# Expert stage of a fused AdaLN / DeltaNet / MoE kernel: three tiles of output rows ahead of the second half of the FF columns, the odd slot in the first half, pair rows numbered by partition

## The reference, cut to what matters

```python
capacity = int(1.25 * N * K / E) + 1                 # N = 2048, K = 2, E = 8: 641 slots
k_probs, k_idx = jax.lax.top_k(softmax(xf @ router_w.T), K)
k_probs = k_probs / jnp.sum(k_probs, axis=-1, keepdims=True)
...                                                  # rank of each (token, k) in its expert; rank >= capacity is dropped
buf = jnp.zeros((E, capacity, H)).at[flat_e, slot].add(dispatched)
h = jax.nn.silu(jnp.einsum('ech,ehf->ecf', buf, w1))        # w1: 8 x 128 x 512
out_buf = jnp.einsum('ecf,efh->ech', h, w2)                 # w2: 8 x 512 x 128
pair_out = out_buf[flat_e, slot] * keep[:, None]
combined = jnp.sum(pair_out.reshape(N, K, H) * k_probs[..., None], axis=1)
return combined.reshape(B, T, H) + x
```

## Time and profile before

| | us |
|---|---|
| median of 3 runs | 432.74 |
| the runs | 432.74, 430.11, 435.56 |
| span of the profiled execution, first to last instruction | 396.5 |
| span of the experts in it, first up to the last product's end | 295.65 to 374.3 |
| from there to the end | 22.2 |

### The profile page before, as it was taken

How to read it: one execution, slowest core, us unless ns; L and a number is a source line. 1 busy time by engine, 2 the same in 40 slices (tenths; PEclk the granted TensorE clock), 3 DMA queues, 4 the chain that set the end, 5 groups by cost and what they waited for, 6 DMA issues and landing times.

```text
span 396.5 us, 11509 instructions
## 1 busy us (share of the span) xinstructions
PE 262.7 (66%) x4483; PEld 206.4 (52%) x4483; DVE 218.4 (55%) x760; ACT 104.2 (26%) x212; POOL 169.8 (43%) x165
## 2 busy tenths in 40 slices
PE   2945777866757748558767586373139999999700
PEld 0534454765544637344556465262128888888600
DVE  5576374876591984773795755256323443333425
ACT  1325213335113145122235130001203333333200
POOL 1223234542348460437581336631622555555523
PEclk9965557558556567755665855555558999999955
DMA  7980000000001000001000000000122243532055
GB/s 243 337 317 0 2 3 2 7 2 2 2 12 49 3 2 2 3 3 42 17 3 2 2 3 29 29 4 0 40 92 77 94 137 92 151 94 80 25 170 156
DMA packets 18687, 23.08 MB, mean 58 GB/s; under 512 B 2535, under 2 KB 13048, under 8 KB 18642
## 3 DMA queue, kind: packets, MB, share of 16 engines
q1 hardware_dynamic: 16306, 18.17, 14.4%
q0 software_dynamic: 2336, 4.24, 3.3%
HBM read 11.83 MB, written 11.10 MB: 58 GB/s over the span
## 4 chain that ended last, share of the span: by engine, by line
PE 44%; issue 23%; DVE 15%; POOL 7%; DMA 5%; ACT 3%; SPq 1%; DVEq 1%; POOLq 0%; ACTq 0%
PE ps L1616 9%; PE ps L1633 9%; PE ps L1453 7%; PE ps L1348 5%; PE ps L1333 5%; PE ps L1418 3%; POOL arena L626 2%; PE ps L1499 2%; DMA wmod<-in_wmod 2%; DMA arena<-pair_out 2%; DVE x L1039 2%; POOL arena L647 1%; PE ps L1436 1%; POOL rstd L574 1%; DVE msk L1073 1%
## 5 line engine op out<-in xcount | busy, mean ns | idle before, releaser
L706 POOL DMA_INDIRECT pair_out<-arena,meta x40 | 39.0, 975 | 48.6 <-DVE arena L1275 38.9
L1333 PE MATMUL ps<-const,arena 128*128 128x128 f32 x125 | 25.6, 350 | 28.4 <-DMA arena<-dispatched 11.8
L881 ACT ACTIVATE arena<-ps 128x384 f32<-128x384 f32 x64 | 26.2, 439 | 61.8 <-PE ps L1616 56.3
L1453 PE MATMUL ps<-arena,kT 32*32 32x128 f32 x512 | 24.1, 380 | 23.2 <-DVE wts L1015 14.6
L591 POOL DMA_INDIRECT dispatched<-row,idx x32 | 31.6, 988 | 17.8 <-issue 10.1
L1616 PE MATMUL ps<-arena,w1t 128*128 128x257 f32 (+1 forms) x128 | 38.5, 456 | 1.1 <-DVE arena L1259 1.1
L636 POOL TENSOR_TENSOR s_mk<-s_sb,const 128x512 f32<-128x512 f32 x16 | 21.2, 1325 | 40.8 <-ACT s_sb L792 40.8
L1633 PE MATMUL ps<-w2t,arena 128*128 128x128 f32 x320 | 37.0, 275 | 0.0
L1633 PEld LDWEIGHTS ps<-w2t,arena 128*128 128x128 f32 x320 | 36.4, 192 | 0.0
L1333 PEld LDWEIGHTS ps<-const,arena 128*128 128x128 f32 x125 | 18.8, 178 | 32.4 <-DMA arena<-dispatched 11.8
L1418 PE MATMUL ps<-v,wts 32*32 32x9 f32 x2048 | 28.3, 191 | 7.3 <-issue 7.3
(11 more groups left out here) (173 smaller groups left out, 511.5 us busy)
## 6 DMA issues: line engine op xcount, KB each, us to landing
dispatched<-fill SPq DMA_DIRECT2D x12, 260.0 KB, 4.9
arena<-dispatched SPq DMA_DIRECT2D x9, 325.0 KB, 3.4
w1t<-in_w SPq DMA_DIRECT2D x8, 256.0 KB, 2.9
w2t<-in_w SPq DMA_DIRECT2D x8, 256.0 KB, 2.9
pair_out<-zero SPq DMA_DIRECT2D x4, 512.0 KB, 6.4
arena<-pair_out SPq DMA_DIRECT2D x4, 512.0 KB, 5.7
out<-arena SPq DMA_DIRECT2D x4, 256.0 KB, 2.3
const<-in_constants SPq DMA_DIRECT2D x1, 790.0 KB, 6.6
```

What stands on the lines that cost most here:

```text
L706: pool.indirect_dma_start(pair_d, bass.IndirectOffsetOnAxis(ap=meta[:, u, a, 0:1].bitcast(U32), axis=0), orow[:, u, a, :], None, bounds_ch ...
L881: a_.activation(hid[:, u, f, c0:c0 + cn], ps[:, k % 4, 0:cn], ACT.Silu).then_inc(hid_done[u].sem, 1)
L1333: return nc.tensor.transpose(out, in_, ident[0:in_.shape[0], 0:in_.shape[0]])
L1453: f = mm(ps[j * BLK:(j + 1) * BLK, 2 * (hg % 2) + w, hg // 2 * P:(hg // 2 + 1) * P], st[r, t * P + j * BLK:t * P + (j + 1) * BLK], mv_[r, ...
```

## The change

Each expert is done in another order on TensorE: five of the eight up products (the first half of the slots for all four f, and one of the second half), the output tiles 0 to 2, the transposes for the next expert, the other three up products, tile 3 with the odd slot's product, tile 4. The odd slot moves to column 0 of `bT` and `hid`, so the first half is 385 columns and the second 256, and its four operations on VectorE come ahead of row product 0. The transposes get the banks 4 and 5 and the output tiles a ring of two, 6 and 7: tile a waits for the row product of tile a - 2. VectorE copies `meta` and the transposes behind row product 2. The last loop step is written out: no ninth expert is loaded or transposed, and the scatter of the odd rows goes ahead of that of tile 4. In SyncE's queue the wait for the even expert's scatters goes ahead of the wait and load for `w1t[1]`. The id of a pair becomes `32 * p + 8 * g + 2 * t + k` for partition p, group g and tile t, so a partition's pairs of a group are one run of 4 KB in `pair_out`, at a step of 16 KB from partition to partition.

```diff
-CH = (CT + 1) // 2 * P
+FA = (CT + 1) // 2
+CH = 1 + FA * P
 NHALF = [(0, CH), (CH, CAP - CH)]
 FT = FF // P
+UPS = [(f, n) for n in range(2) for f in range(FT)]
+UPS_A = FT + 1
+LAST_AT = CT - 2
...
-    c[:, COL["pid"]] = (TOPK * tok + np.arange(TOPK)[None, None, :]).reshape(P, -1)
+    c[:, COL["pid"]] = (PAIRS // P) * r + np.arange(TG * TOPK)[None, :]
...
-    pair_v = pair_d.rearrange("(g t p k) c -> g p t (k c)", t=TG, p=P, k=TOPK)
+    pair_v = pair_d.rearrange("(p g n) c -> g p (n c)", g=GROUPS, p=P)
...
-            return ps[:, 4 + (u * CT + a) % 4, :]
+            return ps[:, 6 + (u * CT + a) % 2, :]
+
+        def rows_made(a):
+
+            return a + 1 + (a > LAST_AT)
...
+                outs_gone(0, i)
                 sp.wait_ge(up_ps[1].sem, up_ps[1].now(i))
                 sp.dma_start(w1t[:, 1, :], w1_v(i * 2 + 3)).then_inc(w1_in[1].sem, 16)
-                outs_gone(0, i)
...
-            next_slots(0, NE // 2 - 1)
-            outs_gone(0, NE // 2 - 1)
...
+            with pool.Fori(0, NE // 2 - 1) as i:
+                rows_out(0, i, 0, CT)
+                rows_out(1, i, 0, CT)
+            rows_out(0, NE // 2 - 1, 0, CT)
+            rows_out(1, NE // 2 - 1, 0, CT - 1)
             pool.wait_ge(s_lastR, 2)
             pool.indirect_dma_start(pair_d, ...)
+            rows_out(1, NE // 2 - 1, CT - 1, CT)
...
+                    for k, (f, n) in enumerate(UPS):
+                        c0, cn = NHALF[n]
+                        act.wait_ge(up_ps[u].sem, up_ps[u].now(i, k + 1))
+                        if k == 0:
+                            act.wait_ge(r_ps[u].sem, r_ps[u].before(i))
+                            act.wait_ge(last_done[u].sem, last_done[u].before(i))
+                        a_.activation(hid[:, u, f, c0:c0 + cn], ps[:, k % 4, 0:cn], ACT.Silu).then_inc(hid_done[u].sem, 1)
...
-                    v_.tensor_scalar(pid[:], pid[:], float(GT * TOPK), None, ALU.add).then_inc(pid_next.sem, 1)
+                    v_.tensor_scalar(pid[:], pid[:], float(TG * TOPK), None, ALU.add).then_inc(pid_next.sem, 1)
...
-                    dve.wait_ge(outs_left[u].sem, outs_left[u].before(i))
                 for a in range(lo, hi):
                     dve.wait_ge(r_ps[u].sem, r_ps[u].now(i, a + 1))
...
-                dve.wait_ge(hid_done[u].sem, hid_done[u].now(i))
+                dve.wait_ge(hid_done[u].sem, hid_done[u].now(i, FT))
...
+            def expert(u, i, after):
+
+                last_products(u, i)
+                rows(u, i, 0, FA)
+                if after:
+                    slot_meta(*after[:2])
+                    slots_T(*after)
+                rows(u, i, FA, LAST_AT + 1)
+                last_out(u, i)
...
+            with dve.Fori(0, NE // 2 - 1) as i:
+                expert(0, i, (1, i, i * 2 + 1))
+                rows(0, i, LAST_AT + 1, CT)
+                expert(1, i, (0, i + 1, i * 2 + 2))
+                rows(1, i, LAST_AT + 1, CT)
+            i = NE // 2 - 1
+            expert(0, i, (1, i, NE - 1))
+            rows(0, i, LAST_AT + 1, CT)
+            expert(1, i, None)
             dve.wait_ge(s_lastO, 1)
             v_.tensor_scalar(lastR[:], T4[0:NE, 0:P], lastx[:, DM + 1:RW], None, ALU.mult).then_inc(s_lastR, 2)
+            rows(1, i, LAST_AT + 1, CT)
...
+            def down(u, i, lo, hi):
+
+                if lo == 0:
+                    pe.wait_ge(w2_in[u].sem, w2_in[u].now(i))
+                for a in range(lo, hi):
+                    if a >= 2:
+                        pe.wait_ge(r_done[u].sem, r_done[u].now(i, rows_made(a - 2)))
+                    else:
+                        made_ = CT + (a if a + 1 < 2 else 1)
...
+            def expert(u, i, after):
+
+                up(u, i, 0, UPS_A)
+                down(u, i, 0, FA)
+                if after:
+                    slots_T(*after)
+                up(u, i, UPS_A, len(UPS))
+                down(u, i, FA, LAST_AT + 1)
...
+            with pe.Fori(0, NE // 2 - 1) as i:
+                expert(0, i, (1, i))
+                down(0, i, LAST_AT + 1, CT)
+                expert(1, i, (0, i + 1))
+                down(1, i, LAST_AT + 1, CT)
+            i = NE // 2 - 1
+            expert(0, i, (1, i))
+            down(0, i, LAST_AT + 1, CT)
+            expert(1, i, None)
+            down(1, i, LAST_AT + 1, CT)
+            pe.wait_ge(r_done[1].sem, r_done[1].now(i, rows_made(LAST_AT) + 1))
             tr(T4[0:NE, 0:P], lastO[:]).then_inc(s_lastO, 1)
```

More of the change, by code:

```diff
@@ L433, in program @@
         r_ps = [event(f"rows_ps{u}", CT, "pe") for u in range(2)]
-        last_done = [event(f"last_products{u}", FT) for u in range(2)]
+        last_done = [event(f"last_products{u}", FT, "dve") for u in range(2)]
         r_done = [event(f"rows_done{u}", CT + 1, "dve") for u in range(2)]
@@ L874, in _ @@
                 for u in range(2):
-                    for f in range(FT):
-                        for n, (c0, cn) in enumerate(NHALF):
-                            k = 2 * f + n
-                            act.wait_ge(up_ps[u].sem, up_ps[u].now(i, k + 1))
-                            if k == 0:
-                                act.wait_ge(r_ps[u].sem, r_ps[u].before(i))
-                            a_.activation(hid[:, u, f, c0:c0 + cn], ps[:, k % 4, 0:cn], ACT.Silu).then_inc(hid_done[u].sem, 1)
+                    for k, (f, n) in enumerate(UPS):
[5 more added lines that the diff above has]
+                        a_.activation(hid[:, u, f, c0:c0 + cn], ps[:, k % 4, 0:cn], ACT.Silu).then_inc(hid_done[u].sem, 1)
         @block.vector
@@ L1598, in slots_T @@
                 for a in range(CT):
[L1599 removed]
+                    f = tr(ps[:, 4 + a // 4, (a % 4) * P:(a % 4 + 1) * P], xb[:, u, a, 0:DM])
                 f.then_inc(bT_ps[u].sem, 1)
[L1602 to L1616 removed]
@@ L1618, in down, with up @@
-            def down(u, i):
-                pe.wait_ge(w2_in[u].sem, w2_in[u].now(i))
-                if u:
-                    pe.wait_ge(r_done[0].sem, r_done[0].now(i))
-                else:
-                    pe.wait_ge(r_done[1].sem, r_done[1].before(i))
-                for a in range(CT):
-                    if a >= 4:
-                        pe.wait_ge(r_done[u].sem, r_done[u].now(i, a - 3))
+            def up(u, i, lo, hi):
+                if lo == 0:
+                    pe.wait_ge(w1_in[u].sem, w1_in[u].now(i))
+                    pe.wait_ge(bT_done[u].sem, bT_done[u].now(i))
+                for k in range(lo, hi):
+                    f, n = UPS[k]
+                    c0, cn = NHALF[n]
+                    if k >= 4:
+                        pe.wait_ge(hid_done[u].sem, hid_done[u].now(i, k - 3))
+                    elif u:
+                        pe.wait_ge(hid_done[0].sem, hid_done[0].now(i, 5 + k))
+                    else:
+                        pe.wait_ge(hid_done[1].sem, hid_done[1].before(i, 5 + k))
+                    mm(ps[:, k % 4, 0:cn], w1t[:, u, f * P:(f + 1) * P], bT[:, u, c0:c0 + cn], start=True, stop=True).then_inc(up_ps[u].sem, 1)
@@ new lines, in down @@
+            def down(u, i, lo, hi):
+                if lo == 0:
+                    pe.wait_ge(w2_in[u].sem, w2_in[u].now(i))
+                for a in range(lo, hi):
+                    if a >= 2:
+                        pe.wait_ge(r_done[u].sem, r_done[u].now(i, rows_made(a - 2)))
+                    else:
+                        made_ = CT + (a if a + 1 < 2 else 1)
+                        if u:
+                            pe.wait_ge(r_done[0].sem, r_done[0].now(i, made_))
+                        else:
+                            pe.wait_ge(r_done[1].sem, r_done[1].before(i, made_))
@@ L1635, in down @@
+                    if a == LAST_AT:
                         pe.wait_ge(last_done[u].sem, last_done[u].now(i))
@@ L1637, in down @@
                     m.then_inc(r_ps[u].sem, 1)
+            def expert(u, i, after):
[5 more added lines that the diff above has]
+                down(u, i, FA, LAST_AT + 1)
             slots_T(0, 0)
             pe.wait_ge(s_lastx, 16)
[L1641 to L1651 removed]
+            tr(T6[:, 0:NE], lastx[:, 0:DM]).then_inc(s_lastT, 1)
+            with pe.Fori(0, NE // 2 - 1) as i:
[9 more added lines that the diff above has]
+            pe.wait_ge(r_done[1].sem, r_done[1].now(i, rows_made(LAST_AT) + 1))
             tr(T4[0:NE, 0:P], lastO[:]).then_inc(s_lastO, 1)
```

82 lines of the change are left out of this document (20 added, 62 removed).

## The result

| | median us | runs | ratio to before, 95% interval |
|---|---|---|---|
| kernel before | 433.26 (430.11 to 435.56) | 4 | |
| changed kernel | 421.57 (420.72 to 421.70) | 4 | 0.9722, 0.9679 to 0.9765 |

The profiled execution of the changed kernel spans 419.7 us and took 421.5 us: 1.8 us lie outside the span, not 36.

What follows compares the result with a forecast made beforehand. TensorE's stream was taken to bound the experts, GpSimd's scatters, the pair load and VectorE's sums the tail. Terms 2.10 − 1.37 + 0.23 − 0.41 = +0.55 us gave span 397.0, with 36.2 outside it 433.3 us; range 430.2 to 436.2.

Steps and rivals of the forecast that it cites:

- The step that failed: Outside the profiled span: the 36.2 us between it and the median of 432.74 were carried over unchanged.
- TensorE as the path through the experts: Experts stage: up to the last expert TensorE's stream sets the time, 9.57 us an expert; every wait adds.
- The stall at tile 2: Each expert's output rows: tile 2 waits for VectorE to free tile 0's bank, 0.30 us each, +2.10 over seven.
- The rival without a stall: Output rows: tile 0's bank is released in time for tile 2; sum −2.10, 431.2 us, chance 20%.
- Tiles 0 and 1 wait for no Silu, and tile 3 for no bank: Output rows in each expert: Silus and row 1's release come in time, so no further wait is added.
- The head start of the scatters: Last expert: its first scatter starts 5.85 us into the expert instead of 7.22, −1.37 us.
- The rival that it is absent: Last expert: scatters wait for tile 3 or odd rows, or row 0 is released no earlier; 434.7 us, chance 8%.
- The pace of the last scatters: Last expert: six scatters follow at 1.278 us each, odd rows fifth, tile 4 last, each arriving in time.
- the longer last transfer: Tail: the last scatter moves a full tile, 2.2 us to landing instead of 1.97 for eight rows, +0.23 us.
- The pair load: Tail: pair rows load in 4 KB runs instead of 1 KB, at 395 GB/s instead of 358, −0.41 us.
- The rivals with a load as fast as before, or slower: Tail's pair load: no faster, 433.7 us, chance 18%; or slower at 290 GB/s, 434.7 us, chance 12%.
- Late scatters: Experts: pair rows 16 KB apart make scatters land late and lengthen each of seven steps; 444 us, chance 2%.

Runs made afterwards that it cites:

- e1_before: Kernel before, unchanged, run again on chip 2: 399.78 us against 400.77, ratio 0.998.
- e2_after: Changed kernel, unchanged, run again on chip 2: 402.90 us against 400.77 for the kernel before, ratio 1.0065.
- e16_before_4: Kernel before, unchanged, on chip 12: 424.71 us against 426.11, ratio 1.000.
- e15_rows_first_4: Changed kernel with row products 0 and 1 ahead of the odd slot's operations, chip 12: 415.22 us against 426.11 for the kernel before, ratio 0.9765.
- both with the copies: Kernel before and changed kernel, each with 22 DRAM-to-DRAM copies of 512 KB in each of three attention-loop groups, chip 8: 452.25 and 444.95 us.
- e5: Changed kernel with row products 0 and 1 ahead of the odd slot's operations, chip 3: 398.78 us against 400.05 for the kernel before, ratio 0.9965.
- e4: Changed kernel with the old pair ids and pair load, so the new order alone, chip 2: 401.79 us against 400.77 for the kernel before, ratio 1.005.

## Why the prediction was wrong

The two conditions side by side, each span cut at the second and the eighth up:

| profile | to first up | first expert | six experts | from the eighth up on | span |
|---|---|---|---|---|---|
| e1_before, chip 2 | 297.06 | 11.20 | 57.33 | 32.01 | 397.6 |
| e2_after, chip 2 | 294.76 | 12.75 | 60.37 | 30.62 | 398.5 |
| e16_before_4, chip 12 | 310.41 | 11.89 | 66.03 | 33.37 | 421.7 |
| e15_rows_first_4, chip 12 | 312.96 | 11.99 | 58.11 | 29.94 | 413.0 |
| changed kernel, first measurement | 316.23 | 12.29 | 60.37 | 30.81 | 419.7 |

**The step that failed** is the last of the sum: "The 36.2 us between that span and the median of 432.74 lie outside it and stay." In every run here 1.8 to 2.2 us lie outside the span. So nearly all of the 36 us were execution that the profile of before didn't have: that profile looks like those of the chips at 400 us, and the times lie near those of the chips where TensorE's signals come late. From e1 to e16 the span grows by 24.1 us, 13.4 of them ahead of the experts and 8.7 in six experts. And so they did not stay. On one chip, 8, both with the copies, the changed kernel takes 7.3 us less, −6.3 us of its profile in six experts and −2.8 from the eighth up on. In the table the changed kernel's first measurement has 5.7 us less than e16 in six experts (66.03 − 60.37) and 2.6 less in the last stretch (33.37 − 30.81), where 1.55 were forecast. These are two chips beside each other, and the whole spans differ by 2.0 us only, since the stretch ahead of the experts is 5.8 longer in the changed kernel. The kernel before has no profile where it takes 433 us, 7 to 8 us more than on chips 8 and 12. So 8.2 of the 11.7 us can be placed, if the stretch ahead of the experts is left out; the rest, and what the kernel before took there on the first measurement's chip, are not traced. On one chip, 12, the version with the rows first gains 10.9 us by the medians; its spans differ by 8.7: +2.6 ahead of the experts, +0.1 in the first, −7.9 in six, −3.4 behind.

**TensorE as the path through the experts:** right on the trace it was read from, wrong for the times. Where the time is 425 us, TensorE waits in up for the ring of four banks, 1.45 us an expert.

**The stall at tile 2:** right in mechanism and place; the term was mis-sized. 0.30 an expert was forecast and 0.50 came (10.06 − 9.56): 0.27 instead of 0.20 for the restart, a release that comes later in some experts, and the fillings at each change between rows and up. Over seven steps this is +3.5 us instead of +2.10. Put into the sum, 0.55 + 1.4 = 1.95 us (2.2 with the head start as measured below); measured on the four chips +1.6. The rival without a stall falls.

**Tiles 0 and 1 wait for no Silu, and tile 3 for no bank:** right; in the chains of e2 nothing stands between them.

**The head start of the scatters:** −1.11 (7.22 to 6.11) instead of −1.37. The rival that it is absent falls. **The pace of the last scatters** and **the longer last transfer**: right; from the last scatter's start to SyncE's load it is 2.27 us with the full tile last (404.04 − 401.77, the same in e2), 2.05 with the eight odd rows last in e1 (381.38 − 379.33): +0.22, forecast +0.23.

**The pair load:** right; −0.35 over fifteen profiles, forecast −0.41, with 396 to 411 GB/s where 395 was assumed (e5 apart). The 395 came from writes of 2 KB runs, so that it fits is in part luck. The rivals with a load as fast as before, or slower, fall, though single executions of the kernel before differ by up to 0.4 in it (12.90 to 13.27 unchanged), and e4 and e2, which differ in the numbering alone, by 0.01. In the new order VectorE waits for the load no more. By the rule from the Trainium skill, DMA: Bandwidth & Descriptors, "Where 436 GB/s comes from", as I used it, nothing would have been gained; the rates of 396 to 411 GB/s don't agree with that.

**Late scatters**, the rival on the other side, did not appear.

In short, the sum was right to about 1 us (+0.55 against +1.6) for chips on which the kernel before takes 400 us, and had nothing on the condition in which it was timed. That this condition exists, no row of the one profile could show. The 36 us were the hint: 9% of a time that no record covers asks for a cause before it is carried over as a constant.

## What to carry to other kernels

Compare the span of a profiled execution with the time; all nineteen profiled executions that carry their own time have 1.8 to 2.2 us outside the span, and where 36 were missing the two came from different conditions, so that the sum made in one didn't hold in the other. A stream with 0.83 us of slack in its ring of banks is tight only as long as each signal is on time. Here an order that changes more often between up and rows cost 1.6 us on chips where all is on time and saved 7 to 12 where it isn't; the traces show where it saves (the results of up come on time and no ring wait follows), not what makes them late, so another kernel may not repeat it. And whoever shrinks a ring has to look at what its releaser does first: two row products ahead of the odd slot's four operations gave back 0.44 us an expert, and made the version with the lowest times (0.9965, 0.9965, 0.9765).

## What was not expected of the hardware

- One and the same program takes 400 us on four chips and 425 to 433 us on others, with a granted clock that doesn't tell them apart (0.67 to 0.71 over all executions on the first, 0.66 to 0.70 on the others) and the main instructions as long (a scatter 974 ns in e1 and 976 in e16, a Silu 439 and 441). The difference is in waits.
- Where it is slow, TensorE has waits of 1.9 to 6.3 us in the attention loop, each behind 32 or 48 instructions of the same line, that no engine and no queue of the profile ends (14.0 to 17.1 us in all), and other engines see its results late: by up to 2.2 us in up in the old order, by up to 1.1 for tile 3 in the new one, and once by 0.4 in the new order's up. Whether both have one cause is open; so is the cause.
- "issue" and "remote" are not causes. The 0.58 us of "issue" in e16_before_4 end 0.05 behind a Silu which frees the bank that the product needs.
